# One bias row inside the value buffers instead of selector matmuls, in a two-layer graph network kernel

## What is computed

```python
h = jnp.maximum(_layernorm(x, axis=-1), 0.0)
x = x + _L0_gnn_ref(h, adj, ...)   # two graph convolutions, then LSTMs over windows of 1, 2, 3 and 4 nodes
h = jnp.maximum(_layernorm(x, axis=-1), 0.0)
x = x + _L1_gnn_ref(h, L1_gnn_W, adj, L1_gnn_bias)

def _L1_gnn_ref(x, W, adj, bias):
    adj_0 = jnp.diag(jnp.diagonal(adj))
    adj_1 = jnp.triu(adj, k=1)
    adj_2 = jnp.tril(adj, k=-1)
    h = jnp.einsum('bjf,kfo->kbjo', x, W)
    out = (jnp.einsum('ij,bjo->bio', adj_0, h[0]) + jnp.einsum('ij,bjo->bio', adj_1, h[1])
           + jnp.einsum('ij,bjo->bio', adj_2, h[2]))
    return out + bias[None, None, :]
```

## Time and profile before

| what | value |
|---|---|
| median of 3 runs | 407.77 us |
| lowest, highest | 407.67, 408.24 us |
| the profiled execution, its time | 407.99 us |
| the profiled execution, its span | 406.2 us |
| granted TensorE clock, mean | 1.00 of full speed |
| instructions in the profile | 6535 |

### The profile page before, as it was taken

How to read it: one execution, slowest core, us unless ns; L and a number is a source line. 1 busy time by engine, 2 the same in 40 slices (tenths; PEclk the granted TensorE clock), 3 DMA queues, 4 the chain that set the end, 5 groups by cost and what they waited for, 6 DMA issues and landing times.

```text
span 406.2 us, 6535 instructions
## 1 busy us (share of the span) xinstructions
PE 398.6 (98%) x2401; PEld 347.5 (86%) x2401; DVE 338.2 (83%) x858; ACT 287.5 (71%) x579; POOL 40.9 (10%) x43
## 2 busy tenths in 40 slices
PE   8999999999999999999999999999999999999997
PEld 7787889898887889899777889899797788989775
DVE  5668999997989689887998788988898767788795
ACT  4767775685897676777588676777589677766553
POOL 4910003000200003000110000300110000000140
DMA  7820000000000000000000000000000000000003
GB/s 228 310 111 2 1 0 2 1 2 0 2 1 27 1 27 0 27 2 0 3 0 26 27 0 27 1 27 2 0 2 27 26 2 26 2 27 2 1 0 131
DMA packets 5215, 11.18 MB, mean 28 GB/s; under 512 B 1088, under 2 KB 2112, under 8 KB 4672
## 3 DMA queue, kind: packets, MB, share of 16 engines
q1 hardware_dynamic: 5184, 10.77, 7.5%
HBM read 6.57 MB, written 4.19 MB: 27 GB/s over the span
## 4 chain that ended last, share of the span: by engine, by line
PE 84%; DVE 10%; ACT 3%; DMA 1%; issue 1%; POOL 0%; SPq 0%; DVEq 0%; ACTq 0%
PE PS L500 11%; PE PS L509 11%; PE PS L501 11%; PE PS L528 6%; PE PS L573 6%; PE PS L525 6%; PE PS L524 6%; PE PS L449 4%; PE PS L459 4%; PE PS L426 4%; PE PS L441 4%; PE PS L563 3%; PE PS L564 3%; PE PS L565 3%; PE PS L552 2%; ACT TC L835 1%
## 5 line engine op out<-in xcount | busy, mean ns | idle before, releaser
L829 ACT ACTIVATE GT<-PS,BG 128x256 f32<-128x256 f32 (+2 forms) x312 | 158.0, 564 | 17.2 <-PE PS L528 12.0
L500 PE MATMUL PS<-HH,WIH 128*128 128x256 f32 (+2 forms) x312 | 107.8, 346 | 1.7 <-DVE HH L977 1.7
L501 PE MATMUL PS<-HH,WIL 128*128 128x256 f32 (+2 forms) x312 | 102.7, 330 | 0.0
L509 PE MATMUL PS<-HL,WIH 128*128 128x256 f32 (+2 forms) x294 | 97.4, 331 | 0.1
L835 ACT ACTIVATE TC<-CS 128x512 f32<-128x512 f32 (+2 forms) x88 | 45.2, 514 | 49.2 <-DVE CS L953 36.0
L500 PEld LDWEIGHTS PS<-HH,WIH 128*128 128x128 f32 x312 | 58.8, 188 | 10.1 <-DVE HH L984 2.9
L368 POOL TENSOR_TENSOR RS<-VE,NHALF 128x4 f32<-128x4 f32 (+2 forms) x17 | 29.2, 1719 | 353.8 <-DVE VE L901 353.8
L501 PEld LDWEIGHTS PS<-HH,WIL 128*128 128x128 f32 x312 | 58.9, 189 | 4.1 <-issue 1.2
L509 PEld LDWEIGHTS PS<-HL,WIH 128*128 128x128 f32 x294 | 55.5, 189 | 6.1 <-DVE HL L992 1.9
L528 PE MATMUL PS<-SL,WHH 128*128 128x256 f32 (+2 forms) x192 | 60.1, 313 | 0.1
L524 PE MATMUL PS<-SH,WHH 128*128 128x256 f32 (+2 forms) x192 | 59.8, 312 | 0.0
(11 more groups left out here) (96 smaller groups left out, 652.8 us busy)
## 6 DMA issues: line engine op xcount, KB each, us to landing
out_tbd<-X SPq DMA_DIRECT2D x15, 256.0 KB, 2.0
X<-x_tbd SPq DMA_DIRECT2D x3, 1024.0 KB, 12.9
X<-x_tbd SPq DMA_DIRECT2D x4, 256.0 KB, 4.5
WI<-wih_t SPq DMA_DIRECT2D x1, 1024.0 KB, 5.8
WH<-whh_t SPq DMA_DIRECT2D x1, 768.0 KB, 7.3
out_tbd<-X SPq DMA_DIRECT2D x2, 128.0 KB, 1.7
WL<-w_l SPq DMA_DIRECT2D x1, 192.0 KB, 6.5
WG<-wg SPq DMA_DIRECT2D x2, 64.0 KB, 3.4
```

The lines of the kernel that those rows point to most:

```text
L500: pe.matmul(dst, WIH[:, p - 1, cols], x_high, start=True, stop=False)
L501: pe.matmul(dst, WIL[:, p - 1, cols], x_high, start=False, stop=False)
L509: mm = pe.matmul(dst, WIH[:, p - 1, cols], x_low, start=False, stop=(j == 0))
L829: act.activation(GT[:, s, q, 0:n], bank(s, q)[:, 0:n], ACT.Tanh if q == C else ACT.Sigmoid, bias=BG[:, 4 * (p - 1) + q:4 * (p - 1) + q + 1 ...
```

## The change

In `ADJ2` the row is the source node and the column the output node. The lower side takes only sources with a number below the output's, so row 127 of `ADJ2[:, 1, :]` is zero for all outputs. The change sets this row to one, and keeps the bias in row 127 of the third value of both value buffers. The lower side product then adds the bias by itself. For that

- the selector matmuls, `TWO`, `BIAS`, `BIASH`, `BIAS2`, their load, memsets, split and row copy go; the upper side product opens the bank (`start=True`);
- `copy_value` copies the first two values in one instruction, 128 partitions by 256 columns, and the third in another, 127 partitions by 128 columns, so that row 127 stays; only the second raises `value_sb`;
- GpSimd writes the row of ones with a third affine select, which waits for the first two;
- SyncE, after its loads and ahead of the stores, waits for the last split of the LSTM's raw weights and loads the bias four times side by side into row 127 of each buffer; TensorE waits for both before graph 1.

```diff
             for g in range(1, GROUPS):
                 sp.dma_start(X[:, g * G:(g + 1) * G, :], x_tbd[:, g * G:(g + 1) * G, :]).then_inc(x_rest, 16)
...
+            sp.wait_ge(split_w, 2 * (2 * POOL_SKIPS - 1))
+            sp.wait_ge(late_low, 2)
+            for w in (WI, WH):
+                sp.dma_start(w[T - 1:T, SIDES, :].rearrange("a (b n) -> a b n", b=PACK),
+                             bias.rearrange("(a b n) -> a b n", a=1, b=1).broadcast_to([1, PACK, D])).then_inc(bias_row, 16)
...
-            pool.memset(TWO[:, :].bitcast(F32), 0.0).then_inc(bias_parts, 1)
-            pool.wait_ge(bias_parts, 1)
-            pool.memset(TWO[0:2, :].bitcast(F32), 1.0).then_inc(bias_parts, 1)
...
+            pool.wait_ge(consts, 6)
+            pool.affine_select(out=ADJ2[:, 1, :], in_=ADJ2[:, 1, :], compare_op=ALU.is_gt, fill=1.0,
+                               base=T - 1, pattern=[[0, T]], channel_multiplier=-1).then_inc(consts, 1)
...
                 if k == 0:
-                    pe.matmul(as_batches(ps)[:, lo:hi, :], TWO[:, :],
-                              BIAS2[:, :].unsqueeze(1).broadcast_to([T, hi - lo, D]), start=True, stop=False)
                     pe.wait_ge(value_sb, G * g + q * PACK + hi)
                 mm = pe.matmul(ps[:, lo * D:hi * D], ADJ2[:, k, :], values(q)[:, 1 + k, lo * D:hi * D],
-                               start=False, stop=(k == SIDES - 1))
+                               start=(k == 0), stop=(k == SIDES - 1))
...
-            pe.wait_ge(consts, 6)
-            pe.wait_ge(w_late, 48)
+            pe.wait_ge(consts, 7)
+            pe.wait_ge(w_late, 32)
             pe.wait_ge(late_low, len(LATE_ORDER))
-            pe.wait_ge(bias_parts, 3)
+            pe.wait_ge(bias_row, 32)
...
-            def late_bias_row():
-
-                act.wait_ge(late_high, len(LATE_ORDER))
-                act.wait_ge(late_low, len(LATE_ORDER))
-                act.activation(BIAS2[0:1, :], BIASH[0:1, :].bitcast(F32), ACT.Copy).then_inc(bias_parts, 1)
...
                 act.wait_ge(value_mm, G * g + n + 1)
-                act.activation(values(q)[:, 0:PARTS, b * D:b * D + D],
-                               ps[:, 0:PARTS * D].rearrange("p (k e) -> p k e", k=PARTS), ACT.Copy,
-                               scale=RS2[:, n:n + 1]).then_inc(value_sb, 1)
+                act.activation(values(q)[:, 0:SIDES, b * D:b * D + D],
+                               ps[:, 0:SIDES * D].rearrange("p (k e) -> p k e", k=SIDES), ACT.Copy,
+                               scale=RS2[:, n:n + 1])
+
+                act.activation(values(q)[0:T - 1, SIDES, b * D:b * D + D], ps[0:T - 1, SIDES * D:PARTS * D], ACT.Copy,
+                               scale=RS2[0:T - 1, n:n + 1]).then_inc(value_sb, 1)
```

More of the change, by code:

```diff
@@ L126 @@
 POOL_SKIPS = 3
[L127 to L130, removed]
+LATE_HIGH_AT = {6: ("wi",), 7: ("wh",), 16: ("wl",)}
+LATE_LOW_AT = {7: ("wi",), 9: ("wh",), 18: ("wl",)}
+LATE_ORDER = ("wi", "wh", "wl")
 CELL_EARLY = (1, 2, 15)
@@ L189, in program @@
         BG1 = sb("BG1", [T, D])
[L190 to L193, removed]
         BI = sb("BI", [D, 16])
@@ L256, in program @@
         rs2 = sem("rs2")
-        bias_parts = sem("bias_parts")
+        bias_row = sem("bias_row")
         turned_up = sem("turned_up")
@@ L295, in late_parts @@
                 return WH[:, POOL_SKIPS - 1, :], WHH[:, POOL_SKIPS - 1, :], WHL[:, POOL_SKIPS - 1, :]
-            if what == "wl":
-                return WL1[:, :, :], WLH[:, :, :], WLL[:, :, :]
-            return BIAS[:, :], BIASH[:, :], BIAS2[:, :]
+            return WL1[:, :, :], WLH[:, :, :], WLL[:, :, :]
         def values(q):
@@ L334, in _ @@
             sp.dma_start(DIAG[:, :], adj_diag).then_inc(w_late, 16)
-            sp.dma_start(BIAS[:, :], bias.rearrange("(a n) -> a n", a=1).broadcast_to([T, D])).then_inc(w_late, 16)
             for g in range(1, GROUPS):
@@ L746, in late_split_high @@
                 else:
-                    act.wait_ge(w_late, 48)
+                    act.wait_ge(w_late, 32)
                 act.activation(high, w, ACT.Copy).then_inc(late_high, 1)
-            def late_bias_row():
-                act.wait_ge(late_high, len(LATE_ORDER))
-                act.wait_ge(late_low, len(LATE_ORDER))
-                act.activation(BIAS2[0:1, :], BIASH[0:1, :].bitcast(F32), ACT.Copy).then_inc(bias_parts, 1)
             def turn_up(g, q, ps):
@@ L841, in units @@
                         late_split_high(what)
-                    if plan is None and k == LATE_ROW_AT:
-                        late_bias_row()
                     if more and k in LN_RELU_AT:
```

## The result

The changed kernel takes 410.23 us, the median of six runs (410.04 to 410.46); the kernel before, in six runs beside it, 407.88 (407.67 to 408.24). The ratio is 1.006, with an interval of 1.0049 to 1.007: slower by 2.4 us, where +1.55 was forecast (409.3 us, range 407.3 to 411.3). The profiled execution took 410.46 us with a span of 408.4, so it is 2.2 us of span that the two traces have to account for. Three executions were far longer than all the others of their kernel (2217.66 us in experiment 1, 992.87 in experiment 4, 432.59 of the kernel before) and stand outside the ratios.

A forecast was written before the change was run, and what follows sets the result against it. TensorE was busy 398.6 of 406.2 us, with ScalarE full in part of graph 1 and waited for at the end. End +1.9, graph 1 +0.45, graphs 2 and 3 -0.4 each: +1.55 on 407.77, 409.3 us, range 407.3 to 411.3.

The forecast's parts named there:

- The price of the second copy: Each value copy on ScalarE: a 128-column copy takes 360 ns and holds 0.25 us; splitting adds d = 0.14 us per value.
- The prices of 0.05 and 0.19: Cheap and dear bounds for d, the added us per value: fixed part mostly hidden, or 128-column activations at some 0.29 us.
- The end: After the last LSTM unit: four quads each 0.48 us later, +1.9 us in all, from +0.6 to +2.9.
- removing the selector gives nothing here: Quads at the end: TensorE is ready by 392.56, or 392.33 without the selector, and waits for the value copies anyway.
- that chain doesn't contain the selectors either: Last quad: copies, VectorE's own-row product and the last two additions form a chain without selectors, moving by 0.48 us.
- Graph 1: Four pairs delay ScalarE 0.56 us; the value matmul waits for the turned states' low half: +0.45 us, selector saving lost.
- Graphs 2 and 3: Two selectors gone (0.46 us) in each, turned states ready 0.35 us later: -0.4 us for each graph.
- Six selectors that save nothing: Selectors of sums 1 and 2 in each of three graphs, ahead of a TensorE wait: counted 0, at most -1.4.
- The rest, taken at nothing: GpSimd's affine select, graph 0's dropped bias instructions, the bias row loads and copies in recurrent units: counted as 0.
- Rival (1): TensorE's time counts and the copies hide: eleven selectors give 2.5 us, so 407.2, or 405.9 us; chance 0.12.
- Rival (2): Second copy is cheap (d = 0.05): end +0.6, graph 1 +0.1, graphs 2 and 3 -0.46 each, 407.6 us; chance 0.22.
- Rival (3): Copies dear (d = 0.19 and more), graph 1's wait repeats in graphs 2 and 3: +3.15, 410.9 us; chance 0.18.

The follow-up runs named there:

- experiment 1: Kernel before, selectors kept, each value copied in two instructions (256 and 128 columns, all 128 partitions): 410.55 us against 407.73, ratio 1.0068.
- experiment 4: Changed kernel with two copies only in the last 20 values, the others copied in one without the bias: 409.20 us against 407.73, ratio 1.0036.
- experiment 2: Changed kernel with one 384-column copy per value, no selectors, bias left out: 407.09 us against 407.73 for the kernel before, ratio 0.9982.
- experiment 6: Changed kernel with four spare 384-column matmuls ahead of the wait for the values in group 3's quads 0 to 2: 410.24 us, ratio 1.0065.
- experiment 9: Changed kernel with one spare 128x128 VectorE instruction in graph 0, where the bias's split stood: 409.94 us against 407.59, ratio 1.006.
- experiment 7: Changed kernel with one copy, no selectors and no ones row; GpSimd adds the bias to each quad of X: 413.26 us, ratio 1.014.
- experiment 8: Kernel before, with bias row and two copies, no selector, only in group 1 and group 2's quads 0 to 2: 407.40 us, ratio 0.9996.

## Why the prediction was right, and where it was off

The direction, its cause and the range were right: the split costs more than the selectors give, and experiments 1 and 2 show both halves by themselves, +2.8 and -0.6 us. The sum was 0.8 to 0.9 us too low (410.23 or, by the ratio, 407.77 x 1.006 = 410.2, against 409.3). Point by point:

- **The price of the second copy** (d = 0.14). As a duration 370 to 386 ns came, for 360; as a hold, 0.25, exactly the slope's value, and 0.61 to 0.62 for the pair. The prices of 0.05 and 0.19 are both out for a pair in a row. The Trainium skill, ScalarE: Activation LUTs, What ACT_TABLE_LOAD costs, has figures that make an estimate of 387 ns for 128 columns, near the measured 386 and 370 ns. With the overlap of 93 ns that it states, the hold would be an estimated 0.29, and the trace has 0.25: a copy of 0.36 to 0.41 us is overlapped by the next for 0.11 to 0.16.
- **The end** (forecast +1.9, measured +2.2). The step that was mis-sized is "0.48 us later". The four pairs took 2.60 us and not 2.55, since the copies grow longer towards the end of a row (0.36 to 0.41 us), which makes +0.53; experiments 1 and 6 have just this number. (Where the prediction gives the end as 2.1 us beside the other price, its own sum says 1.9.) Another 0.06 to 0.10 came from the selector's absence: "removing the selector gives nothing here" was too kind, as TensorE, idle for longer, starts 0.15 us after the copy instead of 0.05. Everything did move along in these three: no quad hid any of it. In the last quad it is 0.41, and there "that chain doesn't contain the selectors either" was wrong. The chain of the kernel before ends in them:
```profile
402.62 0.12 PE PS L570
402.74 0.88 PE PS L573 x4
403.61 0.02 issue
403.64 0.42 DVE X L1057
```
VectorE's own-row product did start 0.53 us later after the first copy's start (404.56 against 401.92; before, 402.29 against 400.18). But the second addition had waited for TensorE's second half, with a selector in it; now it doesn't, and the two additions take 0.83 us instead of 0.93. Experiment 2's gain of 0.14 in this quad is mostly the same thing.

- **Graph 1** (forecast +0.45, measured +0.64). The stall is at the instruction, and on the tile, that was named. Two numbers were small: the low half came 0.62 us late instead of 0.56 (125.24 against 125.12, in a graph that had begun 0.50 earlier), and the matmul starts 0.14 us after the low half is there (126.07 against 125.93), not 0.05. The selector ahead of the stall saved nothing, as forecast: -0.02 in experiment 2.
- **Graphs 2 and 3** (forecast -0.4 each, measured -0.29 and -0.27). Two selectors saved in each was right, 0.47 and 0.44 with one copy. The copies took back 0.17 of it, not 0.06, at the place that was named. The errors there partly cancel, which was luck: the low half is ready at 221.49, in a graph that began 0.16 later, so it came only 0.22 later than before and not 0.35; but TensorE starts 0.15 after it instead of 0.05, and the matmul behind it follows after 0.25 us (221.64 to 221.89) instead of 0.18 before.
- **Six selectors that save nothing**: right. The matmul at 144.84 is at 144.99 now, behind the same chain (its low half ends at 144.94), and experiment 2 has no gain outside graphs 2 and 3.
- **The rest, taken at nothing.** The load of the bias row, the affine select and graph 0 cost nothing that the trace shows (graph 0 is 0.05 longer). Two effects were not seen: the idle 0.46 us at the entry (+0.36), and -0.25 us in the convolutions before graph 1. They come with the change, though not by its steps; together they add 0.1.

By term, the miss in the profiled execution is +0.3 at the end, +0.2 in graph 1, +0.25 in graphs 2 and 3, some +0.15 for the two new effects and graph 0, and -0.28 from the start-up, which no run ties to the change. Rival (1), that TensorE's time counts, fell in experiment 2: seventeen selectors gave 0.6 us. Rival (2), cheap copies, fell with the hold of 0.25. Rival (3), at +3.15, lies as far above the measured 2.35 as the forecast lies below it. Its price for a copy was wrong. Its second half was not: the wait of graph 1 does repeat in graphs 2 and 3 and takes back 0.17 us in each, about midway between the forecast's 0.06 and this rival's 0.26.

Still open: why the 0.46 us arise at the entry, since experiment 9 shows only that they go with an instruction more in VectorE's stream. Experiment 7's kernel has no such idle time either; there VectorE has as few instructions as in the changed kernel but 16 waits more. That the loading of VectorE's instructions falls on another place is a possible cause that no run tests. Open too is the -0.25 in the convolutions, which every kernel made from the changed one has (with experiment 9, -0.19; with experiment 7, whose entry is clean, -0.26) and the two with the bias's VectorE split don't. So this effect does not need the one at the entry. TensorE is busy without a gap there in both; the eight matmuls of L441 take 3.60 instead of 3.73 us and the 32 of L449 3.83 instead of 3.95. A link to VectorE's stream is a guess.

## What to carry to other kernels

Work that only fills a time in which its engine waits anyway gives nothing when it goes: ask at each place of an operation what its engine does next, and for how long it would stand. Here 3.7 us of matmuls were worth 0.6, and one extra ScalarE instruction of 0.25 us, repeated 64 times, cost nothing in most places, yet 2.8 us where ScalarE was full or was the last link; when an operation is split, count its price as a hold of the engine, and only for the last one of a row as the time until its result, at just those places. If both forms are open, they can be chosen per place, as in experiment 8, which took back the loss but gained nothing that could be measured.

## What the runs showed of the hardware that was not expected

- **TensorE starts later after a longer stand.** The side product starts 0.05 us after the last copy's end where TensorE had stood for 0.41 us or less (experiments 1 and 6), and 0.15 us after it where it had stood for 0.73. The value matmuls that wait for a low half don't follow this: 0.14 us after graph 1's stall of 0.31, and 0.15 in graph 2 (221.64 against 221.49), where the list shows no stand of the matmul. So the length of the stand alone does not decide it; what does is open.
- **VectorE pays for GpSimd.** A cast of 128x512 went from 0.43 to 1.40 us beside a GpSimd addition of the same size, a product from 0.69 to 1.00 us, and `add_own`'s product from 0.75 to 1.78 us (experiment 7).
- **0.46 us of idle VectorE with nothing to wait for** went with one instruction placed 295 us earlier (experiment 9).
- **The partition count has no price**: 127x128 and 128x128 copies take the same 386 and 370 ns into the one and the other value buffer.
